# Graph attention over an edge list, one Trainium2 core: rows of one node and four edges, two to a partition, instead of rows of eight; the mixer's pair sums taken from K transposed times K

## The chip, the cores and the metric

The kernel runs on one core of one Trainium2 chip. The metric is the device time of one execution in microseconds (us).

## What is computed

A graph of N = 3125 nodes with F = 256 features has 50,000 pairs of nodes. Each pair is an edge in both directions, each node has an edge to itself, so there are E = 103,125 edges (`src`, `dst`), sorted by `dst`. The layer is a graph attention with a feed-forward net, a dense mixer over all nodes, and a mixture of experts:

```python
xn = layernorm(x)
q = xn @ Wq;  k = xn @ Wk;  v = xn @ Wv                  # 4 heads of 64
e = sum(k[src] * q[dst], per head) / sqrt(256)           # one number per edge and head
a = softmax of e over the edges that share a dst
ft = segment_sum(v[src] * a, dst)                        # then + xn, norm, ffn, norm
# mixer, 8 heads of 32: kn, qn normalised; vN = [1, v] / N
kv_mod[i, j, e] = sum_n kn[n, i] * kn[n, j] * vN[n, e]
y = 0.5 * sum_ij qn_i qn_j kv_mod[i, j] + scale^2 * qn @ kv + scale^4 * sum(vN)
y = y[..., 1:] / y[..., :1]
x = x + graph(xn) + mixer(xn)
x = x + experts(layernorm(x))                            # 8 experts, two per node
```

For the column e = 0 of `kv_mod`, where vN is 1/N, the sum over nodes of kn_i kn_j is an entry of K transposed times K.

## The kernel before

The work is in six stages, one after the other, each a block in which every engine has its own hand-written list of instructions, with semaphores between them. A stage begins when all engines have ended the one before.

**`stage_project`** (0 to about 100 us) normalises x, writes the table `kv_tab` (k and v of each node, 512 numbers, 2 KB a row) and `q_tab` to HBM, and works out on VectorE where each row of edges lies. The sorted edges are cut into blocks of L = 8. A *row* is a block of edges together with one node: where a block's eight edges reach into several nodes, it has a row for each, and the edges of other nodes are masked (`foreign`). This gives at most NB - 1 + N rows with NB = 12,891, in TILES = 126 tiles of 128 rows. The table `t3` in HBM says for each block which edges it holds.

**`stage_edges_and_mix`** (to 1443 us) goes over the tiles. For each tile n:

- SyncE loads 128 entries of `t3` (`load_blocks`, L2266 to L2270: one DMA of 127 rows and one of a single row) and 128 rows of q (`q_win`, L817).
- VectorE makes a comparison matrix (`compare`, L845), TensorE finds from it each row's block and node (`find`, L1219 to L1222), ScalarE turns these into the indices `idx`, the mask `foreign` and the spreading matrix (`settle`, L1110 to L1116). This runs AHEAD = 4 tiles ahead.
- GpSimd gathers k and v of the source nodes: 8 indirect DMAs per tile, one per edge slot of the 128 rows (L804, 256 KB each), into a ring of RING = 4 tiles. It waits for `idx` and, four tiles back, for the last reader of the ring's place.
- TensorE spreads q over the rows (`q_of_rows`, L1229). VectorE multiplies k by q in two halves of four slots (`times_q`, L855, into `prod`) and adds up per head (`add_up`, L862), masks (L869), takes the row's own maximum (L874) and subtracts it (L879). ScalarE takes exponentials (`exps`, L1121 to L1124).
- VectorE weighs v of four slots (`weigh`, L884), ScalarE v of the other four (`weigh_slot`, L1132, 16 instructions). VectorE adds its four by two folds (`fold` L892, `fold_on` L897), ScalarE's four by a reduction (`sum_act` L902), and the two sums (`fold_last` L910) into `part`, which goes to HBM (`parts`, 130 KB per tile).

Between these stand the mixer's instructions, cut into 477 micro-steps, four to a tile (`micro_steps`), so that they end seven tiles ahead of the last. Nine micro-steps are one window u of 125 nodes: first 26 rounds on K, V (`k_first`, `k_last`: for each head an outer product of pairs `kf_ps`, squared by ScalarE, L1164, and summed over the nodes by matmuls against v, L1269, and against a column of 1/N, L1270), then 13 steps of coefficients (`coef`), then 26 rounds on Q (L1324, L1344, L1346, squares at L1171). The order on each engine, the same for each tile, is written out at the end of its block: on VectorE

```python
for n in range(TILES + 1):
    # c = 0: times_q(n, 0)  times_q(n, 1)        c = 1: add_up(n, 0)  add_up(n, 1)
    # c = 2: keep_own(n)  weigh(n - 1)  top(n)  less_top(n)  fold(n - 1)
    # c = 3: compare(n + 5)  fold_on(n - 1)  sum_act(n - 1)  fold_last(n - 1)
```

(with three stretches of the micro-step `mix(n, c, ...)` around them).

**`stage_merge`** (to about 1587 us) first rescales rows of the same node to a common maximum, by scans along the rows (L1556 to L1575, one row of 128 numbers per tile and head), and then walks N_STEPS = TILES + NT - 1 = 150 steps, each a tile of rows added into a window of 125 nodes: SyncE loads the 130 KB of the tile (L1436), GpSimd scales them (L1528), ScalarE makes a selection matrix in two instructions (`mark`, L1512, L1515), TensorE multiplies (L1495, one fp32 product, two records), VectorE adds to `acc` (L1588). Every six steps VectorE loads six window numbers into registers.

`stage_graph_ffn`, the routing and `stage_experts` follow and are not touched, apart from the place of a buffer.

## Time and profile before

| | us |
|---|---|
| median of 3 executions | 2294.39 (2288.54 to 2297.39) |
| span of the profiled execution | 2291.0 |
| first gather of `stage_edges_and_mix` | 107.3 |
| last gather begins | 1423.8 |
| steps of `stage_merge`, first matmul to last add | 1467.3 to 1585.2 |

Of the profiled execution the page gives its span, 2291.0 us, and no separate time; what lies around the span is taken as the distance to the median of the executions, 3.4 us. The span is the time from its first instruction to its last. A busy share of an engine is its share of that span or of the window named; a DMA share is the mean over the core's 16 DMA engines.

### The profile page before, as it was taken

How to read it: one execution, taken by the hardware profiler on the slowest of the kernel's cores; microseconds unless marked ns; L12 is line 12 of the kernel's file. 1: busy time of each engine (PE TensorE's matmuls, PEld its weight loads, DVE VectorE, ACT ScalarE, POOL GpSimd, SP SyncE). 2: the span in 40 equal slices, each digit the busy share in tenths (PEclk: the TensorE clock that was granted, in tenths of full speed). 3: DMA queues.
4: the chain of work that ended last, by engine and by line, in shares of the span. 5: the costliest groups of instructions: out<-in, count | busy, mean ns of one | idle time of the engine just before them, and what ended most of it. 6: DMA issues, size and time to landing. Idle time of an engine off the chain costs nothing. (4 is left out here: it accounts for less than half of the span.)

```text
span 2291.0 us, 44322 instructions
## 1 busy us (share of the span) xinstructions
PE 1830.8 (80%) x12285; PEld 1291.9 (56%) x12285; DVE 1833.5 (80%) x3705; ACT 1525.4 (67%) x5228; POOL 1257.2 (55%) x1281
## 2 busy tenths in 40 slices
PE   7767788887786688787888771487999679999996
PEld 4433333333333566666666650244988579999995
DVE  7389999999999999999999999555899854444442
ACT  2267777778877587887888875687555255555553
POOL 0177777777777577777777776375000024444442
PEclk9879999889987688988989985698999789999998
DMA  8577777777777677777878787474001282222223
GB/s 229 182 230 232 231 230 235 233 224 228 228 226 228 182 230 239 235 234 237 237 232 242 226 243 211 138 206 119 15 29 32 89 280 38 35 35 36 37 37 77
DMA packets 213272, 394.34 MB, mean 172 GB/s; under 512 B 46354, under 2 KB 140637, under 8 KB 213005
## 3 DMA queue, kind: packets, MB, share of 16 engines
q0 software_dynamic: 91392, 278.99, 43.0%
q1 hardware_dynamic: 96848, 90.41, 13.3%
q10 hardware_dynamic: 24829, 22.64, 3.0%
q8 instruction: 78, 1.28, 0.2%
q14 instruction: 125, 1.02, 0.1%
HBM read 346.47 MB, written 48.65 MB: 172 GB/s over the span
## 5 line engine op out<-in xcount | busy, mean ns | idle before, releaser
L804 POOL DMA_INDIRECT ring<-kv_tab,idx x1008 | 981.0, 973 | 441.0 <-issue 297.6
L1132 ACT ACTIVATE act_val<-ring,act_val 128x64 f32<-128x64 f32 x2016 | 559.2, 398 | 51.0 <-DVE part L910 46.6
L855 DVE TENSOR_TENSOR prod<-ring,tile_bank 128x1024 f32<-128x1024 f32 x252 | 299.4, 1211 | 11.2 <-ACT tile_bank L1121 6.3
L862 DVE TENSOR_REDUCE score<-prod 128x16 f32<-128x1024 f32 x252 | 298.3, 1207 | 0.0
L2149 POOL DMA_INDIRECT x_sum<-e_yw,to_row x56 | 125.0, 2232 | 218.5 <-DVE e_yw L2175 197.2
L2134 POOL DMA_INDIRECT xr<-rows,from_row x56 | 57.6, 1029 | 291.2 <-issue 290.9
L2224 PE MATMUL e_h<-e_xT,e_now 128*128 128x128 f32 x1792 | 211.7, 277 | 0.8 <-DVE e_now L2165 0.8
L2224 PEld LDWEIGHTS e_h<-e_xT,e_now 128*128 128x128 f32 x1792 | 206.9, 194 | 1.3 <-DVE e_now L2165 1.2
L2239 PE MATMUL e_yps<-e_now,e_hT 128*128 128x256 f32 x896 | 202.5, 379 | 0.0
L2189 ACT ACTIVATE e_now<-e_w_all 128x2048 f32 x56 | 106.9, 1912 | 131.2 <-PE e_yps L2239 131.2
L2239 PEld LDWEIGHTS e_yps<-e_now,e_hT 128*128 128x128 f32 x896 | 166.2, 190 | 20.1
L2173 DVE TENSOR_TENSOR e_y<-e_yps,small 128x256 f32<-128x256 f32 x56 | 23.8, 425 | 189.2 <-PE e_yps L2239 182.0
L902 DVE TENSOR_REDUCE act_sum<-act_val 128x260 f32<-128x1040 f32 x126 | 154.5, 1226 | 14.2 <-ACT act_val L1132 14.1
L2197 ACT ACTIVATE e_hT<-e_h,small 128x128 f32<-128x128 f32 x448 | 127.6, 368 | 45.4 <-PE e_h L2224 45.4
L884 DVE TENSOR_TENSOR val<-ring,tile_bank 128x1024 f32<-128x1024 f32 x126 | 152.6, 1211 | 0.0
L1324 PE MATMUL bank_f<-u_T,pair 96*124 96x125 bf16 x800 | 90.1, 245 | 67.3 <-ACT xn_buf L1158 67.3
L1257 PE MATMUL bank_f<-pair,u_T 96*125 96x496 bf16 x200 | 89.6, 448 | 67.0 <-ACT u_T L681 34.3
L1257 PEld LDWEIGHTS bank_f<-pair,u_T 96*125 96x125 bf16 x200 | 28.4, 142 | 199.1 <-ACT phi L1164 77.1
L1229 PE MATMUL tile_bank<-q_win,spread 128*128 128x256 f32 x252 | 95.4, 466 | 38.2 <-DVE val L884 38.1
L1324 PEld LDWEIGHTS bank_f<-u_T,pair 96*124 96x124 bf16 x800 | 67.5, 149 | 102.9 <-ACT xn_buf L1158 74.6
L1270 PE MATMUL bank_f<-phi,one_col 125*32 125x496 f32 x200 | 118.1, 676 | 0.0
L1495 PE MATMUL step_ps<-scaled,hot 128*125 128x260 f32 x300 | 98.2, 436 | 20.7 <-DVE acc L1588 12.9
(425 smaller groups left out, 4794.0 us busy)
## 6 DMA issues: line engine op xcount, KB each, us to landing
loaded<-parts SPq DMA_DIRECT2D x150, 130.0 KB, 2.3
e_w_all<-L_ffn_W SPq DMA_DIRECT2D x16, 1024.0 KB, 12.2
parts<-part ACTq DMA_DIRECT2D x126, 130.0 KB
q_win<-q_tab SPq DMA_DIRECT2D x126, 128.0 KB
ring<-kv_tab,idx POOLq DMA_INDIRECT x1008
kv_tab<-kv_t SPq DMA_DIRECT2D x25, 224.0 KB
xn_buf<-x SPq DMA_DIRECT2D x25, 125.0 KB
x_sum<-x_buf SPq DMA_DIRECT2D x25, 125.0 KB
```

The costliest lines, as they stand in the source:

```text
L804: pool.indirect_dma_start(out=ring[:, n % RING, e, :], out_offset=None, in_=t.kv_tab, in_offset=bass.IndirectOffsetOnAxis(ap=idx[n % 6][:, ...
L855: dve.tensor_tensor(prod[half][:, :, :], ring[:, n % RING, at, 0:F], bcast(q_ps[n % 2].unsqueeze(1), 128, L // 2, F), ALU.mult).then_inc(q ...
L862: dve.tensor_reduce(score[:, at, :], prod[half][:, :, :].rearrange("p s (h d) -> p s h d", h=HG), AX.X, ALU.add).then_inc(reduced, 1)
L884: dve.tensor_tensor(val[n % 2][:, :, :, 0:DG], ring[:, n % RING, 0:L // 2, F:2 * F].rearrange("p s (h d) -> p s h d", h=HG), bcast(w_ps[n ...
L902: dve.tensor_reduce(act_sum[:, :], act_val[n % 2][:, :, :, :].rearrange("p h d s -> p (h d) s"), AX.X, ALU.add).then_inc(sum_ready, 1)
L1132: one = act.activation(act_val[n % 2][:, h, 0:DG, e - L // 2], ring[:, n % RING, e, F + h * DG:F + (h + 1) * DG], ACT.Copy, scale=act_val[ ...
L1270: pe.matmul(normT_ps[beyond, :], one_col[:, 1 - half:1 - half + DM], phi_k[h % 2], start=False, stop=last, skip_group_check=True).then_inc ...
L1324: mm = pe.matmul(qf_ps[k % 2][:, b, :], x.pair3[:, b * PB:(b + 1) * PB], q_.turned_parts[u % 2][:, k, 0:TP], start=True, stop=True)
L2149: pool.indirect_dma_start(out=t.x_sum, out_offset=bass.IndirectOffsetOnAxis(ap=to_row[:, n:n + 1], axis=0), in_=yw[n % 2][:, :], in_offset ...
L2197: gelu = act.activation(hT[j % 2][:, b, :], h_ps[j % 2][:, b, :], ACT.Gelu, bias=small[j][:, b:b + 1])
L2224: mm = pe.matmul(h_ps[j % 2][:, b, :], now1[j % 2][:, k, b * 128:(b + 1) * 128], xT[j % 2][:, k, :], start=(k == 0), stop=(k == FC - 1))
L2239: mm = pe.matmul(y_ps[j % 2][:, 0:F], hT[j % 2][:, b, :], now2[j % 2][:, b, :], start=(b == 0), stop=(b == HB - 1))
```

## The change

1. **Rows.** L is 4 and a new constant G is 2: a block has four edges, and a tile has 128 partitions with two rows each (G * L = 8 slots, as before). NB is 25,782, TILES = ceil((25,781 + 3,125) / 256) = 113, N_STEPS = 137. The gathers are 113 x 8 = 904 for 1008; their size is the same. The entries of `t3` are 40 bytes wide for 72, `load_blocks` issues four DMAs per tile for two, `q_win` is loaded twice per tile (two buffers for three), `parts` has 260 KB per tile.
2. **VectorE in a tile.** `times_q` writes its product over k in the ring. `compare` handles 256 rows in one instruction. `weigh` and `weigh_slot` now each weigh the four slots of one of the two rows, and all go to one buffer `val`, so that one fold over both rows (1040 numbers a partition) and a second (520) give `part`; `sum_act` and `fold_last` are gone. `fold` waits for ScalarE's four slots, and `weigh` waits for `where_read` and `q_ready[0]`, since the banks of PSUM are shared.
3. **Buffers in PSUM** for the q of the rows and for the weights `w_ps` are one per row and one, for two and two; `settle` is cut into `settle_rows` (c = 1) and `settle_nodes` (c = 2), `find` into `find_rows` and `find_nodes`.
4. **Mixer.** Every 16th slot takes two micro-steps (EXTRA = 16), so that 477 of them fit into 113 tiles. The matmuls against the column of 1/N (L1270) are gone; instead `gram_sums` adds K transposed times K of a window (two matmuls per window), and at the coefficients eight matmuls, two products and two reductions on VectorE make the pair sums of it.
5. **Merge.** The scans and their tables are 256 wide. Each step has two selections and two matmuls: the first row's by ScalarE (`mark`) and GpSimd as before, the second row's selection (`mark`) and scaling (`scale`) by VectorE.

```diff
@@ constants
-L = 8
+L = 4
+G = 2
-TILES = -(-(NB - 1 + N) // 128)
+TILES = -(-(NB - 1 + N) // (128 * G))
...
+def micros(n, c):
+    i = 4 * n + c
+    return range(i + i // EXTRA, i + 1 + (i + 1) // EXTRA)
@@ stage_project
+            def rows_of_edges():
+                for e in range(L):
+                    order(dve.tensor_tensor(split(edges[1])[:, :, e], split(edges[1])[:, :, e], blk_i[:, :], ALU.add))
@@ stage_edges_and_mix, gpsimd
-                for e in range(L):
-                    pool.indirect_dma_start(out=ring[:, n % RING, e, :], ...
-                                            ).then_inc(landed[n % RING * 2 + e // (L // 2)], 16)
+                for g in range(G):
+                    for e in range(L):
+                        pool.indirect_dma_start(out=ring[:, n % RING, g * L + e, :], ...
+                                                ).then_inc(landed[n % RING * 2 + g], 16)
@@ stage_edges_and_mix, vector
-                dve.tensor_tensor(prod[half][:, :, :], ring[:, n % RING, at, 0:F], bcast(q_ps[n % 2].unsqueeze(1), 128, L // 2, F),
-                                  ALU.mult).then_inc(q_read, 1)
+                k = ring[:, n % RING, g * L:(g + 1) * L, 0:F]
+                dve.tensor_tensor(k, k, bcast(q_ps[g].unsqueeze(1), 128, L, F), ALU.mult).then_inc(q_read[g], 1)
...
             def weigh(n):
                 dve.wait_ge(w_ready, n + 1)
+                dve.wait_ge(q_ready[0], min(n + 3, TILES))
+                dve.wait_ge(where_read, min(n + 2 + AHEAD, TILES))
...
             def fold(n):
-                dve.wait_ge(exp_ready, n + 1)
-                dve.tensor_tensor(v[:, 0:2, :], v[:, 0:2, :], v[:, 2:4, :], ALU.add).then_inc(folding, 1)
+                dve.wait_ge(act_val_ready, n + 1)
+                dve.tensor_tensor(v[:, :, 0:2 * FD], v[:, :, 0:2 * FD], v[:, :, 2 * FD:], ALU.add).then_inc(folding, 1)
...
-            def sum_act(n):
-                dve.tensor_reduce(act_sum[:, :], act_val[n % 2][:, :, :, :].rearrange("p h d s -> p (h d) s"), AX.X, ALU.add
-            def fold_last(n):
-                dve.tensor_tensor(part[n % 3][:, :], v[:, 0, :], act_sum[:, :], ALU.add).then_inc(folded, 1)
+                dve.tensor_tensor(part[n % 2][:, :, :], v[:, :, 0:FD], v[:, :, FD:2 * FD], ALU.add).then_inc(folded, 1)
@@ stage_edges_and_mix, tensor
+            def gram_sums(u, half):
+                at = slice(half * 128, (half + 1) * 128)
+                pe.matmul(gram_ps[:, half, :], k_.unit[u % 2][:, at], k_.unit[u % 2][:, at], start=False, stop=(u == NT - 1),
...
-                    pe.matmul(normT_ps[beyond, :], one_col[:, 1 - half:1 - half + DM], phi_k[h % 2], start=False, stop=last,
@@ stage_merge, tensor
-                pe.matmul(step_ps[n % 3][:, 0:FD], hot[n % 4][:, :], scaled[n % 3][:, :], start=True, stop=True
+                pe.matmul(step_ps[n % 3][:, 0:FD], hot0[n % 4][:, :], scaled0[n % 3][:, :], start=True, stop=False)
+                pe.wait_ge(hot1_ready, n + 1)
+                pe.wait_ge(scaled1_ready, n + 1)
+                pe.matmul(step_ps[n % 3][:, 0:FD], hot1[n % 4][:, :], scaled1[n % 3][:, :], start=False, stop=True
@@ stage_merge, vector
+            for n in range(N_STEPS):
+                if n % RUN == 0:
+                    window = numbers_of(t.step_w, n, mybir.EngineType.DVE, NT - 1)
+                if n + 1 < N_STEPS:
+                    mark(n + 1)
+                    scale(n + 1)
+                dve.wait_ge(step_ready, n + 1)
+                wait(dve, step_read, n)
+                at = t.acc[:, window[n % RUN], :]
+                dve.tensor_tensor(at, at, step_ps[n % 3][:, 0:FD], ALU.add).then_inc(step_read, 1)
```

How the order on VectorE moves, at two places. First a tile in the K rounds of `stage_edges_and_mix`. Before (`bank_l`, `slv_acc` and `u_` are the mixer's):

```order
L855 TENSOR_TENSOR prod1<-ring,tile_bank0 128x1024
L862 TENSOR_REDUCE score<-prod0 128x16
L862 TENSOR_REDUCE score<-prod1 128x16
L869 SCALAR_TENSOR_TENSOR own<-foreign4,score 128x32
L884 TENSOR_TENSOR val1<-ring,tile_bank0 128x16x64
L874 TENSOR_REDUCE m_all<-own 128x4
...
L879 TENSOR_TENSOR less0<-own,m_all 128x32
L892 TENSOR_TENSOR val1<-val1 128x520
L845 TENSOR_SCALAR later1<-iota,blocks3 128x128
L897 TENSOR_TENSOR val1<-val1 128x260
L902 TENSOR_REDUCE act_sum<-act_val1 128x260
L910 TENSOR_TENSOR part0<-val1,act_sum 128x260
```

and now:

```order
L883 TENSOR_TENSOR ring<-ring,tile_bank1 128x4x256
L888 TENSOR_REDUCE score<-ring 128x4x4
...
L897 SCALAR_TENSOR_TENSOR own<-marks,score 128x32
L914 TENSOR_TENSOR val0<-ring,tile_bank0 128x16x64
L902 TENSOR_REDUCE m_all<-own 128x8
L907 TENSOR_TENSOR less1<-own,m_all 128x32
L871 SCALAR_TENSOR_TENSOR later0<-place,blocks3 128x256
L922 TENSOR_TENSOR val0<-val0 128x2x520
L928 TENSOR_TENSOR part0<-val0 128x520
```

The six instructions from `less` on are four, and the first fold stands after `compare`. Second, the steps of `stage_merge`, before:

```order
L1588 TENSOR_TENSOR acc<-acc,step_ps2 125x260
L1431 TENSOR_LOAD step_w
L1588 ISA
L1588 TENSOR_TENSOR acc<-acc,step_ps0 125x260
L1588 ISA
L1588 TENSOR_TENSOR acc<-acc,step_ps1 125x260
```

and now (`hot` is the second row's selection, `scaled` its scaled parts, which lie in `g_ring`):

```order
L1497 TENSOR_LOAD step_w
L1667 TENSOR_SCALAR hot11<-iota,local 128x125
L1662 TENSOR_TENSOR scaled11<-g_ring,m_weights 128x260
L1683 ISA
L1683 TENSOR_TENSOR acc<-acc,step_ps0 125x260
L1667 TENSOR_SCALAR hot12<-iota,local 128x125
L1662 TENSOR_TENSOR scaled12<-g_ring,m_weights 128x260
```

VectorE has three instructions per step where it had one.

## Rows read from the trace of the kernel before

**Rows 1.** The page: busy time of each engine; the span in 40 slices of 57.3 us.

```profile
PE 1830.8 (80%) x12285; PEld 1291.9 (56%) x12285; DVE 1833.5 (80%) x3705; ACT 1525.4 (67%) x5228; POOL 1257.2 (55%) x1281
DVE  7389999999999999999999999555899854444442
POOL 0177777777777577777777776375000024444442
```

**Rows 2.** Windows of the edge stage: length, busy time and instructions per engine, PEclk, DMA share, GB/s.

```profile
200.00:466.00 266.00, 213.66 (x908) 83.84 (x909) 262.60 (x462) 205.92 (x770) 202.63 (x209) 0.91 0.79 232
486.00:700.00 214.00, 169.93 (x727) 67.69 (x727) 210.06 (x370) 165.36 (x615) 159.95 (x162) 0.90 0.77 224
730.00:794.00 64.00, 39.69 (x275) 33.56 (x275) 59.46 (x142) 32.28 (x133) 38.07 (x41) 0.55 0.66 194
794.00:1320.00 526.00, 428.75 (x4606) 338.04 (x4604) 509.03 (x882) 436.78 (x1628) 392.05 (x406) 0.88 0.79 234
1330.00:1380.00 50.00, 30.60 (x317) 23.46 (x313) 46.83 (x73) 38.10 (x148) 38.12 (x40) 0.82 0.81 244
```

**Rows 3.** One line of the source: the gathers, L804, and GpSimd's waits for the ring.

```profile
L804 POOL DMA_INDIRECT ring<-kv_tab,idx x1008: 940/946/1617, 107.3 to 1423.8; - x168
  issue: 297.6, 961
  ACT act_val L1132: 33.1, 27
```

**Rows 4.** Groups of VectorE: shapes, count, busy us, mean ns, idle before.

```profile
L855 DVE TENSOR_TENSOR prod<-ring,tile_bank 128x1024 f32<-128x1024 f32 x252 | 299.4, 1211 | 11.2 <-ACT tile_bank L1121 6.3 <-DMA ring<-kv_tab,idx 3.7 <-issue 0.6
L902 DVE TENSOR_REDUCE act_sum<-act_val 128x260 f32<-128x1040 f32 x126 | 154.5, 1226 | 14.2 <-ACT act_val L1132 14.1
L892 DVE TENSOR_TENSOR val<-val 128x520 f32<-128x520 f32 x126 | 87.2, 692 | 0.0
L910 DVE TENSOR_TENSOR part<-val,act_sum 128x260 f32<-128x260 f32 x126 | 53.4, 424 | 7.5 <-DVE act_sum L902 0.5 <-issue 0.4
L897 DVE TENSOR_TENSOR val<-val 128x260 f32<-128x260 f32 x126 | 52.9, 420 | 0.2
L845 DVE TENSOR_SCALAR later<-iota,blocks 128x128 bf16<-128x128 f32 x126 | 35.4, 281 | 3.0 <-PE tile_bank L1222 3.0
L1736 DVE SCALAR_TENSOR_TENSOR g_ring<-work,mv,gamma 125x256 f32<-125x256 f32 x25 | 11.6, 465 | 0.0
```

**Rows 5.** The stage before the first gather: a window of it.

```profile
20.00:60.00 40.00, 37.04 (x119) 19.81 (x118) 35.32 (x85) 9.03 (x25) 0.00 (x0) 0.96 0.75 227
```

**Rows 6.** The merge's steps: lines with min/median/max ns, first and last start; a window.

```profile
L1588 DVE TENSOR_TENSOR acc<-acc,step_ps x150: 424/425/427, 1468.7 to 1584.8; 125x260 f32 x150
L1528 POOL TENSOR_TENSOR scaled<-loaded,m_weights x150: 613/619/621, 1466.5 to 1582.0; 128x260 f32<-128x260 f32 x150
L1512 ACT ACTIVATE away<-iota,local x150: 365/385/401, 1466.2 to 1581.2; 128x125 f32<-128x125 f32 x150
...
1467.00:1585.20 118.20, 98.23 (x300) 48.60 (x300) 63.71 (x150) 102.92 (x299) 90.54 (x150) 0.95 0.68 190
```

**Rows 7.** Timeline of TensorE's weight loads in the merge: start, duration, instruction.

```profile
1522.20 0.29 PEld L1495 LDWEIGHTS step_ps<-scaled,hot 128*125 128x125 f32 x2 [0.28 <-issue]
1522.78 0.29 PEld L1495 LDWEIGHTS step_ps<-scaled,hot 128*125 128x125 f32 x2 [0.28 <-issue]
```

**Rows 8.** Groups of VectorE that price the second row's selection and the wider scans.

```profile
L394 DVE TENSOR_SCALAR entered<-thr,begin 128x126 f32<-128x126 f32 x1 | 0.3, 284 | 0.0
L1572 DVE TENSOR_TENSOR_SCAN run<-pen,start,m_rows 126x128 f32<-126x128 f32 x4 | 1.6, 467 | 0.0
```

**Rows 9.** Waits of ScalarE between 1000 and 1200 us: total, times, longest.

```profile
ACT phi L1171 <- PE bank_f L1324: 13.6, 7, 3.0
ACT tile_bank L1121 <- DVE less L879: 5.6, 6, 1.3
```

**Rows 10.** One line: SyncE's issue of the second DMA of `load_blocks`, ns.

```profile
L2270 SPq DMA_DIRECT2D blocks<-t x126: 346/1754/3867, 79.5 to 1354.3; - x126
```

More of the change, by code:

```diff
@@ L858, in add_up @@
-            def add_up(n, half):
-                at = slice(half * L // 2, (half + 1) * L // 2)
-                dve.wait_ge(q_read, 2 * n + half + 1)
+                dve.wait_ge(blocks_in[n % NBUF], G * 32 * (n // NBUF + 1))
+                wait(dve, local_found, n - 1)
+                dve.scalar_tensor_tensor(later[n % 2][:, :, :], place[:, :, :], float(128 * G * n),
+                                         bcast(blocks[n % NBUF][:, :, 2 * T3C:].bitcast(F32), 128, G, 128), ALU.add, ALU.is_ge
+                                         ).then_inc(compared, 1)
@@ L1038, in mix @@
                         onto_x(NT - 1)
+            def mix(n, c, stretch):
+                *whole, last = micros(n, c)
+                if stretch == 0:
+                    for i in whole:
+                        for part_of in range(3):
+                            mix_step(i, part_of)
+                mix_step(last, stretch)
             dve.memset(x.k_factor[:, :], SCALE)
@@ L1214, in _, with find_rows @@
+                    if c == 1 and n + AHEAD < TILES:
+                        settle_rows(n + AHEAD)
+            for j in range(2):
+                act.wait_ge(part_out[j], 16 * len(range(j, TILES, 2)))
         @block.tensor
         def _(pe):
[L1216 removed]
+            def find_rows(n):
                 pe.wait_ge(compared, n + 1)
[L1218 to L1222 removed]
```

598 lines of the change are left out of this document (324 added, 274 removed).

## The prediction

> **What bounds the kernel now.** I read the page first, to see which stages there are. VectorE is at nine tenths from the third slice to the 25th and GpSimd at seven tenths over the same slices, then both fall [rows 1]: the edge stage takes well over half of the span, and the other stages have other bounds. So the change is costed by stage.
>
> In the edge stage two engines are nearly equal, and the windows tell which one sets the pace. Between 200 and 466 us GpSimd does 209 gathers in 266 us, 1.273 us each, or 10.18 us for the 8 of a tile. This is almost its own pace: a gather has a median of 0.946 us, and 961 of 1008 have a gap of about 0.3 us before them which the profile puts down to nothing (297.6 us in all) [rows 3]. VectorE is busy in 98.7% of that window and falls behind a little with each tile, until the ring of four tiles is full. From then GpSimd is held back: 162 gathers in 214 us are 10.57 us a tile in the K rounds, 406 in 526 us are 10.36 us in the Q rounds, with VectorE at 98% and 97% [rows 2]. Between 730 and 794 us, the coefficients of the mixer, 41 gathers take 64 us, 11 us more than at 1.296 us. After the mixer's last step the tiles run at 10.0 us (40 gathers in 50 us), 1.25 us a gather, the gather's floor. So **VectorE bounds now by 2 to 4%, and GpSimd stands right behind it.** From 107.3 us, the first gather, to 1424.8 us, one gather after the last one's start [rows 3], it is 1317.5 us, 10.46 us a tile. TensorE (81%) and ScalarE (83%) have some air [rows 2].
>
> In the merge, 150 steps take 118.2 us, 0.79 us a step [rows 6]. ScalarE's two instructions per step (the first of them 0.385 us) leave it busy 103 of the 118 us; TensorE is busy 98, GpSimd 91, VectorE only 64. VectorE has 0.425 us of work per step.
>
> **The edge stage, GpSimd.** 104 gathers go. At 1.273 us they are worth 132 us; this is the floor of the gain if GpSimd keeps its pace and nothing else is slower. Since the tiles were at 10.46 us and not 10.18, more is to be had only as far as VectorE gets out of the way.
>
> **The edge stage, VectorE, per tile.** Gone: `sum_act` 1.226, `fold_last` 0.424, a fold of 520 numbers 0.692, one of 260 0.420, `compare` 0.281; together 3.043 us [rows 4]. Added: the fold of 1040 numbers, the fold of 520 (0.692) and `compare` on 256. From 260 to 520 numbers a fold grows by 0.272 us, so 1040 cost 0.692 + 0.544 = 1.236 us; `compare` is now a scalar-tensor-tensor on 256 numbers, which elsewhere takes 0.465 us. Together 2.393 us, **0.65 us less a tile**. The two products `times_q`, 1.211 us each [rows 4], keep their shape although they now write in place, and so do `add_up` and `weigh`. The mixer has 4.25 micro-steps per tile for 4. A quarter micro-step more is 0.1 us, an estimate: after the mixer's end the tiles run 0.4 to 0.6 us faster with VectorE less busy [rows 2], and a quarter of a fourth of VectorE's mixer work is of that order at most. The sum of durations also overstates what goes, since successive instructions overlap by some hundredths of a us and two of them go with their overlaps: I give 0.1 us back, a choice that no row here prices. That leaves 0.45 us: 10.57 becomes 10.1 in the K rounds, 10.36 becomes 9.9 in the Q rounds. Both are below GpSimd's 10.18, so **GpSimd becomes the bound**, by 1 to 3%.
>
> The value I take is 10.28 us a tile, 1% over GpSimd's pace, for a pair of engines that close will hold each other up at times: 113 x 10.28 = 1162 us. The bounds are 10.0 us (the tiles after the mixer) and 10.57 (the K rounds now). The jolt at the coefficients was 11 us; two products and two reductions of 512 numbers, 0.69 us each as the fold of 520 [rows 4], make it 3 us longer, but the ring is nearly empty behind a GpSimd that bounds, and three tiles of it take most: 5 us (0 to 14). Sum 1167 us for 1317.5: **150 us less**.
>
> Costed at nothing in this stage: the matmuls against the column of 1/N and the two per window that replace them (TensorE has idle time in the K rounds, busy 80% [rows 2]); the second `q_of_rows`, the two more matmuls of `find` (in the Q rounds TensorE goes from 81% to an estimated 92%; without that cover they would cost up to 1 us a tile); the second pair of loads of `t3`, whose second issue alone takes SyncE 1.75 us [rows 10], so some 4.5 us of 10.3 instead of 2.2; `q_win` and `parts`, some 0.26 MB more on 2.4 MB a tile, which takes the DMA share from 0.78 to about 0.87. The tail after the last gather, 18 us, stays.
>
> **The stage before.** `rows_of_edges` and wider tables add a few us to VectorE where it is 88% busy and TensorE 93% [rows 5]. Between 0 and 6 us, I take 3.
>
> **The merge.** Thirteen steps go. Each of the 137 has two products of TensorE. Weight loads of successive products come 0.58 us apart when nothing else holds them [rows 7], so TensorE needs 1.15 us a step: this is the lower bound, 158 us. VectorE gets a selection (0.284 us, a row of 126 numbers [rows 8]) and a scaling of 260 numbers (0.420 [rows 4]) ahead of its add (0.425 [rows 6]): 1.13 us a step, and every six steps the load of the window numbers, ahead of which nothing is prepared. Two engines at 1.15 and 1.13 us again. The upper bound is that GpSimd's scaling (0.619) stands in line with all three: 1.75 us. I take 1.30, near the lower end, since both rows there are of this same loop: 137 x 1.30 = 178 us for 118, **60 us more**. The 16 scans double their length, at 0.467 us now [rows 8] by at most 7.5 us, and three instructions on 512 numbers go to 1024: **8 us more** (5 to 10) before the first step.
>
> **Sum.** 2291.0 - 150 + 3 + 60 + 8 = 2212 us of span, and with the 3.4 us between span and median **2215 us**, 3.5% less.
>
> **A rule against the change.** GpSimd and VectorE each multiply two operands in SBUF in every merge step, where before VectorE's add had one of its two in PSUM. No row shows the two together: in the merge VectorE's add took 424 to 427 ns and GpSimd's scaling 613 to 621 ns, neither ever disturbed [rows 6]. The Trainium skill (SBUF — State Buffer, Who interferes with whom) says that a VectorE instruction with two SBUF inputs and a GpSimd instruction that reads SBUF share one port, and that the second waits for the whole of the first. By that rule alone the port would need 0.42 + 0.62 = 1.04 us a step and would hide under TensorE; it would cost where the waits line up, which is rival 2.
>
> **The rivals.**
>
> 1. *Lock step, slower than before.* `weigh(n - 1)` now waits for ScalarE's `settle_rows`, this for TensorE's `find_rows`, this stands behind `q_of_rows(n + 1, 0)`, which waits for VectorE's `times_q(n, 0)`; and `fold` waits for ScalarE's last slot. Behind a waiting `weigh` stand `top`, `less`, the exponentials and so ScalarE's next tile. ScalarE is busy 437 of 526 us in the Q rounds, 8.6 us a tile [rows 2], and waits another 0.7 us a tile for TensorE's outer products (13.6 us in 19 tiles [rows 9]); with a quarter micro-step and the wider `settle` that is about 9.9. For it: all three engines are above 90% then. Against it: the waits fall in another third of the tile than the work they wait for, and now ScalarE waits only 5.6 us in 200 for `less`. It decides from (1317.5 - 71 - 5) / 113 = 10.98 us a tile; at 11.6, two hand-offs of some 0.6 us on top of 10.3, the stage takes 1316 us and the whole 2291 - 2 + 71 + 3 = **2363 us**. Chance 0.09.
> 2. *The merge in line.* VectorE and GpSimd take turns, 1.75 us a step: 240 us, 62 more than forecast: **2277 us**. Durations of the two scalings well above 0.42 and 0.62 us would show it. Chance 0.10.
> 3. *Transfers hold the gathers.* In the windows the gathers' own time is 0.97 us on average where the median is 0.946, and some reach 1.617 [rows 3], at a DMA share of 0.78. With 0.87 more of them may. 10.8 us a tile is 1220 us, 58 more: **2273 us**. Against it: at 0.81 the share was highest when the gathers were fastest, 1.25 us each [rows 2]. Chance 0.10.
> 4. *Clean.* Tiles at GpSimd's 10.18 us, 1150 us, no jolt, and TensorE alone in the merge, 158 us: 37 us better, **2178 us**. Chance 0.13.
>
> That the change doesn't do what it says can be left out: the counts of tiles and steps are constants in the program.
>
> **The numbers.** The forecast has the remaining 0.58. The range 2165 to 2295 holds cases 2, 3 and 4 with some room, and leaves out rival 1 and the ends of the unknowns. A measurement of this kernel tells 0.5%, 11 us, from no change. Faster by more than that (below 2283): the forecast, rival 4 and about three fifths of rivals 2 and 3, 0.84. Within it: the rest of these, 0.07. Slower: 0.09.
>
> **What would show each step.** Edge stage: 904 gathers, 8 of them in about 10.2 to 10.3 us, with GpSimd seldom waiting for anything but the 0.3 us, VectorE now waiting for gathers (products idle before on ring landings), folds of 1.24 and 0.69 us, the stage shorter by some 150 us. Merge: TensorE or VectorE above 85% over 137 steps of 1.3 us, VectorE's scaling at 0.42 us. The forecast is wrong if VectorE waits for ScalarE at `weigh` or `fold` by more than half a us a tile, if the gathers' mean rises above 1.05 us, or if the merge's step is above 1.6 us.

## The result, and the profile after

The changed kernel takes **2466.35 us** (median, 2463.6 to 2469.2) against 2295.89 us before: a ratio of **1.0755, 95% interval 1.0738 to 1.0771**. It is 7.6% slower, where 3.5% faster was forecast. The profiled execution has a span of 2464.2 us, 173.2 us more than before. By stage, with the forecast beside it:

| Stage | before | after | change | forecast |
|---|---|---|---|---|
| start to first gather | 107.3 | 120.2 | +12.9 | +3 |
| first gather to last | 1317.5 | 1426.4 | +108.9 | -150 |
| to the merge's first product | 42.2 | 53.4 | +11.2 | +8 |
| steps of the merge | 118.2 | 161.0 | +42.8 | +60 |
| after it | 705.8 | 703.2 | -2.6 | 0 |

So the merge is better than forecast, and the edge stage misses by 259 us. The whole misses the 2215 us of the forecast by 251 us. The page shows where: busy time by engine, then the span in 40 slices of 61.6 us (rows of before: [rows 1]).

```profile
PE 1951.8 (79%) x12642; PEld 1393.1 (57%) x12642; DVE 1757.3 (71%) x3576; ACT 1475.4 (60%) x4781; POOL 1187.8 (48%) x1164
DVE  7378899999998667765666677788799974444442
POOL 0077777777775646544555556155200003444442
```

Up to the 12th slice VectorE is at eight or nine tenths and GpSimd at seven, nearly as before. From the 14th on, where the mixer turns to the queries, VectorE is at five to seven tenths and GpSimd at four to six for ten slices: neither is the bound there. The same windows as in [rows 2] give the sizes:

```profile
200.00:466.00 266.00, 232.04 (x865) 99.44 (x865) 244.01 (x403) 205.10 (x721) 200.68 (x201) 0.91 0.82 247
486.00:700.00 214.00, 186.41 (x735) 80.91 (x736) 202.74 (x336) 173.02 (x608) 163.55 (x162) 0.96 0.82 248
730.00:794.00 64.00, 41.83 (x269) 33.88 (x269) 53.24 (x124) 27.29 (x106) 37.81 (x38) 0.57 0.65 194
794.00:1320.00 526.00, 353.55 (x3523) 270.39 (x3518) 341.54 (x551) 320.45 (x1108) 283.84 (x283) 0.79 0.61 182
```

In the K rounds 201 gathers in 266 us are 10.59 us a tile and 162 in 214 are 10.57: GpSimd sets the pace there (in the first of these windows it waits 4.8 us in all for the ring), but at 10.6 and not at its 10.18 of before. In the Q rounds 283 gathers in 526 us are **14.87 us a tile**, with VectorE busy 65% (before: 10.36 us and 97%) and the clock granted to TensorE at 0.79 for 0.88. That is the loss. One line of the source, the gathers and what GpSimd waited for ([rows 3] before):

```profile
L827 POOL DMA_INDIRECT ring<-kv_tab,idx x904: 940/946/3992, 120.2 to 1545.6; - x181
  issue: 392.1, 850
  ACT val L1160: 232.3, 51
```

Waits for a free place in the ring are 232.3 us for 33.1. The waits of the other engines, each with total, times and longest (TensorE, VectorE twice, SyncE), lead back to the cause:

```profile
PE tile_bank L1273 <- DMA q_win<-q_tab: 193.9, 22, 13.4
...
DVE val L914 <- ACT marks L1137: 134.4, 28, 9.5
DVE val L922 <- ACT val L1160: 91.0, 49, 6.4
...
SPq L846 <- DVE x_buf L1029: 327.0, 23, 19.7
```

VectorE waits for ScalarE at `weigh` and at `fold`, the very chain that rival 1 named; but the chain's head is TensorE, waiting 22 times for a **q window that has not been loaded**, once in most of the 26 rounds on Q. SyncE issues that load, and SyncE waits 23 times for `onto_x` before it may load the next tile of x. SyncE's timeline in one Q round (start, duration, line), and TensorE's row beside it:

```profile
1009.41 0.32 SPq L846 DMA_DIRECT2D xn_buf<-x  x1
1010.70 0.29 SPq L2365 DMA_DIRECT2D blocks<-t  x1
1011.19 2.15 SPq L2366 DMA_DIRECT2D blocks<-t  x1
1014.35 0.27 SPq L2365 DMA_DIRECT2D blocks<-t  x1
1014.81 0.80 SPq L2366 DMA_DIRECT2D blocks<-t  x1
1016.63 1.49 SPq L842 DMA_DIRECT2D q_win<-q_tab  x2
1018.91 0.29 SPq L2365 DMA_DIRECT2D blocks<-t  x1
```

```profile
1022.03 1.22 PE L1273 MATMUL tile_bank<-q_win,spread 128*128 128x256 f32 x2 [8.03 <-DMA q_win<-q_tab]
```

`load_x` stands in SyncE's program ahead of the next tile's `load_q`. It got free at 1009.4, the two pairs of `blocks` took it to 1015.6, the q windows were issued from 1016.6 on, and TensorE's product began at 1022.03, after 8.03 us in which it stood still. A tile's own loads take SyncE 8.2 us (1010.70 to 1018.91) in which it waits for nobody. Before, the same wait was there and cost TensorE 0.2 us in all: q windows were loaded three tiles ahead. Its row in the trace of before:

```profile
SPq L821 <- DVE x_buf L1012: 301.2, 23, 24.1
```

The merge, a window and its VectorE lines ([rows 6] before), and the two folds:

```profile
1600.00:1761.00 161.00, 138.83 (x548) 92.97 (x548) 137.06 (x410) 93.73 (x272) 85.19 (x136) 0.99 0.80 235
```

```profile
L1662 DVE TENSOR_TENSOR scaled<-g_ring,m_weights 128x260 f32<-128x260 f32 x137 | 57.5, 420 | 0.0
L1605 POOL TENSOR_TENSOR scaled<-g_ring,m_weights 128x260 f32<-128x260 f32 x136 | 85.3, 628 | 73.2 <-PE step_ps L1571 72.7 <-DMA g_ring<-parts 0.5
```

```profile
L922 DVE TENSOR_TENSOR val<-val x113: 1221/1241/1276, 149.2 to 1566.0; 128x1040 f32<-128x1040 f32 x113
L928 DVE TENSOR_TENSOR part<-val x113: 677/699/702, 150.5 to 1567.3; 128x520 f32<-128x520 f32 x113
```

A step is 161.0 / 137 = 1.175 us, shorter than the 1.30 of the forecast. The folds cost 1.24 and 0.70 us, as estimated from [rows 4].

### The profile page after: what moved, and what is told of

The parts are those of the page before. It is cut to its first block and busy times, and to the rows that moved or that the text cites. A ratio compares the mean times of both kernels' runs of the same rounds, so it can differ in the third digit from the quotient of the medians.

```text
span 2464.2 us, 45710 instructions
## 1 busy us (share of the span) xinstructions
PE 1951.8 (79%) x12642; PEld 1393.1 (57%) x12642; DVE 1757.3 (71%) x3576; ACT 1475.4 (60%) x4781; POOL 1187.8 (48%) x1164
## 3 DMA queue, kind: packets, MB, share of 16 engines
q14 instruction: 130, 1.06, 0.1%
## 5 line engine op out<-in xcount | busy, mean ns | idle before, releaser
L827 POOL DMA_INDIRECT ring<-kv_tab,idx x904 | 918.5, 1016 | 625.3 <-issue 392.1
L1160 ACT ACTIVATE val<-ring,val 128x64 f32<-128x64 f32 x1808 | 475.7, 336 | 25.7 <-DVE part L928 22.3
L1273 PE MATMUL tile_bank<-q_win,spread 128*128 128x256 f32 x452 | 175.0, 475 | 224.6 <-DMA q_win<-q_tab 193.9
L883 DVE TENSOR_TENSOR ring<-ring,tile_bank 128x1024 f32<-128x1024 f32 x226 | 269.1, 1212 | 15.2 <-DMA ring<-kv_tab,idx 7.8
L888 DVE TENSOR_REDUCE score<-ring 128x16 f32<-128x1024 f32 x226 | 267.8, 1208 | 0.0
L914 DVE TENSOR_TENSOR val<-ring,tile_bank 128x1024 f32<-128x1024 f32 x113 | 137.7, 1218 | 134.7 <-ACT marks L1137 134.4
L1273 PEld LDWEIGHTS tile_bank<-q_win,spread 128*128 128x128 f32 x452 | 87.7, 224 | 246.4 <-DMA q_win<-q_tab 198.5
L922 DVE TENSOR_TENSOR val<-val 128x1040 f32<-128x1040 f32 x113 | 139.9, 1238 | 91.5 <-ACT val L1160 91.0
L1605 POOL TENSOR_TENSOR scaled<-g_ring,m_weights 128x260 f32<-128x260 f32 x137 | 85.9, 628 | 95.0 <-PE step_ps L1571 72.7
L1135 ACT ACTIVATE idx<-tile_bank 128x8 int32<-128x8 f32 x113 | 18.3, 162 | 154.1 <-PE tile_bank L1260 154.1
```

The costliest lines, as they stand in the source:

```text
L827: pool.indirect_dma_start(out=ring[:, n % RING, g * L + e, :], out_offset=None, in_=t.kv_tab, in_offset=bass.IndirectOffsetOnAxis(ap=idx[n ...
L883: dve.tensor_tensor(k, k, bcast(q_ps[g].unsqueeze(1), 128, L, F), ALU.mult).then_inc(q_read[g], 1)
L888: dve.tensor_reduce(score[:, :, g, :], ring[:, n % RING, g * L:(g + 1) * L, 0:F].rearrange("p s (h d) -> p s h d", h=HG), AX.X, ALU.add).t ...
L914: dve.tensor_tensor(val[n % 2][:, 0, :, :, 0:DG], ring[:, n % RING, 0:L, F:2 * F].rearrange("p s (h d) -> p s h d", h=HG), bcast(w_ps.unsq ...
L922: dve.tensor_tensor(v[:, :, 0:2 * FD], v[:, :, 0:2 * FD], v[:, :, 2 * FD:], ALU.add).then_inc(folding, 1)
L1160: one = act.activation(val[n % 2][:, 1, e, h, 0:DG], ring[:, n % RING, L + e, F + h * DG:F + (h + 1) * DG], ACT.Copy, scale=val[n % 2][:, ...
```

## The experiments

Ratios are those on record, each to the kernel before in runs beside it (medians of 2290.8 to 2293.9 us, 2295.9 beside the changed kernel); they are not exactly the quotients of the medians. Where kernels of different batches differ by a few us, the ratios compare them better than the times. "Late x" is the changed kernel with the first edit below; "three repairs" is late x with the first blocks loaded by GpSimd and the merge reading 12 numbers at a time.

| Kernel | us | ratio, 95% interval |
|---|---|---|
| changed | 2466.35 | 1.0755 (1.0738 to 1.0771) |
| late x | 2269.94 | 0.9893 (0.9869 to 0.9918) |
| third q window, x load left | 2286.2 | 0.9953 (0.9929 to 0.9978) |
| before, two q windows | 2390.64 | 1.0419 (1.0396 to 1.0443) |
| late x, rows in 112 + 15 | 2267.65 | 0.9880 (0.9857 to 0.9903) |
| late x, 32 rows of q | 2264.94 | 0.9892 (0.9859 to 0.9925) |
| late x, first blocks by GpSimd | 2248.27 | 0.9830 (0.9804 to 0.9855) |
| late x, merge reads 12 | 2251.78 | 0.9849 (0.9825 to 0.9874) |
| before, mixer part alone | 2291.24 | 1.0002 (0.9992 to 1.0012) |
| **three repairs** | **2237.75** | **0.9758 (0.9739 to 0.9776)** |
| + third q window | 2238.05 | 0.9758 (0.9739 to 0.9777) |
| + one more addition | 2311.64 | 1.0084 (1.0058 to 1.0109) |
| + reductions, slots innermost | 2327.81 | 1.0164 (1.0145 to 1.0183) |
| + second fold moved | 2245.16 | 0.9793 (0.9774 to 0.9813) |
| before, its two repairs | 2292.62 | 1.0000 (0.9989 to 1.0012) |

### SyncE's line: the x load, the third buffer, and the kernel before with two

```diff
@@ sync
-                            if kind == "q" and k == 0 and u + 1 < NT:
+                            if kind == "q" and k == 7 and u + 1 < NT:
                                 load_x(u + 1)
```

> The changed kernel with one edit: SyncE issues the load of the x tile of mixer round u+1 at step 7 of query round u instead of step 0, so its wait on VectorE's addition (step 4) is over when SyncE gets there. Theory A (SyncE's line: the x load waits 327 us in all, 23 times, with the next tile's two q window loads queued behind it, and two q buffers leave no slack): the wait of TensorE for q_win, 193.9 us in the changed kernel, falls under 30 us, the query rounds go from 14.9 us per tile to 11 to 12, and the time from 2466 us to about 2280 (2250 to 2330). Theory B (the two sub-tiles now go through TensorE, ScalarE and VectorE in lock step, and the late window is only where that shows): the query rounds stay above 14 us per tile and the time stays within 30 us of 2466.

It took 2269.94 us, 196 us less. The Q rounds and the gathers of this run (windows, then the group of the gathers: busy us, mean ns, idle before):

```profile
800.00:1280.00 480.00, 415.88 (x4513) 321.71 (x4511) 433.62 (x703) 404.85 (x1415) 366.03 (x355) 0.93 0.83 251
```

```profile
L827 POOL DMA_INDIRECT ring<-kv_tab,idx x904 | 922.4, 1020 | 424.5 <-issue 383.7
```

Now 355 gathers in 480 us are 10.82 us a tile, the ring's wait is 39.6 us, and no wait for `q_win` is left among TensorE's longest. Theory A holds; lock step alone (rival 1) does not, with the same instructions in the same order on TensorE, ScalarE and VectorE.

```diff
@@ x load left where it was
-        q_win = [s.sb(f"q_win{i}", [128, G, F]) for i in range(2)]
+        q_win = [s.sb(f"q_win{i}", [128, G, F]) for i in range(3)]
@@ sync
-                if n + 2 < TILES:
-                    load_q(n + 2)
+                if n + 3 < TILES:
+                    load_q(n + 3)
...
```

The lines left out are the indices and waits of the third buffer, and two small buffers (`own`, `y_inv`) that move to make room.

> The changed kernel with three q window buffers in place of two (loads three tiles ahead), the x load left where it was; y_inv and own move to free columns to make room. Theory A (a late load is what holds the query rounds): the third buffer gives each load one tile more, some 10 us, about the length of the waits (13.4 us the longest for q_win), so most of them go and the time comes near that of the run with the x load moved, 2270 to 2340 us. Theory B (lock step): no change, within 30 us of 2466.

2286.2 us (2268 to 2293 in nine runs): the same loss goes by the other way, most of it.

```diff
@@ kernel before
-        q_win = [s.sb(f"q_win{i}", [128, F]) for i in range(3)]
+        q_win = [s.sb(f"q_win{i}", [128, F]) for i in range(2)]
...
-                    load_q(n + 3)
+                    load_q(n + 2)
...
```

> The kernel before with two q window buffers in place of three and loads two tiles ahead. Theory A: its SyncE waits 301 us for the same x addition, 23 times, so the depth alone brings the waits for q_win there too: the query rounds lengthen and the time goes from 2295 to 2350 to 2450 us. If the doubled loads of the change are needed besides, the time stays within 20 us of 2295.

2390.64 us, 97 us more, and its trace has the changed kernel's wait:

```profile
PE tile_bank L1229 <- DMA q_win<-q_tab: 133.2, 20, 10.8
```

So the depth alone brings the wait. The changed kernel, with its longer line of loads, has more of it (193.9 us for 133.2); how much of that is due to the doubled loads, no run separates.

### Transfers and the long gathers

With the x load moved, a tile is 1228.8 / 113 = 10.87 us: 8.16 of gathers (mean 1.020), 2.35 of gaps of 0.3 us (383.7 us less the 118 ahead of the first gather), 0.35 of waits for the ring. Before it was 7.79 (mean 0.973), 2.36 and 0.26. The gathers themselves are longer, as rival 3 had it. Two runs ask for its cause, the transfers.

```diff
@@ load_blocks, on late x
-        sp.dma_start(to[1:128, g, :], t.t3[ds(first, 127), :])...
+        sp.dma_start(to[16:128, g, :], t.t3[ds(first + 15, 112), :])...
+        sp.dma_start(to[1:16, g, :], t.t3[ds(first, 15), :])...
```

> The run with the x load moved, and the 127 rows of blocks loaded as 112 rows and 15 rows, so that SyncE issues three DMAs for a sub-tile where it issued two. If the 127-row loads crowd few DMA engines and so stretch the gathers (mean 1.011 us in the pair rounds, 0.946 median), GpSimd's 10.6 us per tile there fall by 0.1 to 0.5 us, and the time by 5 to 40 us against that run. If it is only one more DMA on a full SyncE queue, the time is the same or up to 20 us more.

2267.65 us, no difference: the windows of the K rounds are alike (201 gathers in 266 us), and two more issues a tile on SyncE show no cost once its wait is out of the way.

```diff
@@ load_q, on late x; q rows 32 to 127 of a window are left out from the third tile on
-                    sp.dma_start(q_win[n % 2][:, g, :], t.q_tab[ds(first, 128), :])...
+                    rows = 128 if n < 2 else 32
+                    sp.dma_start(q_win[n % 2][0:rows, g, :], t.q_tab[ds(first, rows), :])...
```

> The run with the x load moved, but from the third tile on each q window load brings 32 rows instead of 128 (the other 96 rows of the buffers keep what the first loads left; what is left out is the load of q rows 32 to 127 of a window). It takes 192 KB of some 2.6 MB a tile off the DMA engines. Theory (rival 3 of the prediction: transfers stretch the gathers, mean 1.020 us each where the median is 0.946): the mean falls to 0.96 to 0.99 us, the tile by 0.2 to 0.5 us, the time by 20 to 50 us. Rival (the gathers are long by themselves, by what they move): mean 1.01 or more, time within 8 us of 2270.

The DMA share between 200 and 466 us fell from 0.82 to 0.77 and the gathers did not notice:

```profile
200.00:466.00 266.00, 231.22 (x864) 99.03 (x862) 242.72 (x402) 204.61 (x721) 199.69 (x201) 0.91 0.77 228
```

```profile
L827 POOL DMA_INDIRECT ring<-kv_tab,idx x904 | 924.4, 1023 | 423.6 <-issue 382.6
```

Mean 1.023, time the same (2264.94 us, ratio 0.9892 for 0.9893). Fewer transfers do not shorten the gathers: the cause that rival 3 gave is wrong. What does is in the timeline of late x, GpSimd first and VectorE below:

```profile
869.75 0.95 POOL L827 DMA_INDIRECT ring<-kv_tab,idx  x1 [0.30 <-issue]
871.01 1.57 POOL L827 DMA_INDIRECT ring<-kv_tab,idx  x1 [0.30 <-issue]
872.89 0.95 POOL L827 DMA_INDIRECT ring<-kv_tab,idx  x1 [0.30 <-issue]
```

```profile
870.53 1.23 DVE L922 TENSOR_TENSOR val<-val 128x1040 f32<-128x1040 f32 x1
871.80 0.70 DVE L928 TENSOR_TENSOR part<-val 128x520 f32<-128x520 f32 x1
```

The gather that starts during the fold ends at 872.58, 0.08 us after the second fold. Between 800 and 1000 us, 24 of 147 gathers take over 1.05 us, and 16 of these lie beside both folds. The folds are VectorE's longest instructions of this stage with both operands in SBUF (the next take 0.42 us).

### The folds and the gathers

```diff
@@ on late x: fold (g = 0) and fold_on (g = 1) become
+                dve.tensor_reduce(part[n % 2][:, g, :], v[:, g, :].rearrange("p (s x) -> p x s", s=L), AX.X, ALU.add)
```

> The run with the x load moved, and the two folds of a tile (additions of two operands in SBUF, 1.24 and 0.70 us) replaced by two reductions over the four slots, one for each sub-tile (one operand in SBUF, 1040 numbers each, some 1.2 us each as the products of as many numbers). Theory (shared port): in the trace of the run with the x load moved, the long gathers end 0.05 to 0.1 us after a fold or the fold behind it has ended (gather 871.01 to 872.58, folds 870.53 to 871.76 and 871.80 to 872.50); GpSimd waits for VectorE's additions with two SBUF operands. Without them the gathers' mean falls from 1.020 to 0.96 or 0.97 us, the tile by 0.3 to 0.5 us, the time by 15 to 50 us against 2270, although VectorE works 0.4 us more a tile. Rival: the coincidence means nothing (both wait for the same tile's data); then the gathers keep their 1.02 us and the time stays or rises by up to 15 us.

This run (2791.5 us) and the next three were taken together, beside a kernel before of 2854 us where all other batches have 2291 to 2296, and in their traces TensorE, VectorE and ScalarE stood still together for up to 9.3 us at a time; so their times answer nothing here, and durations are compared within the group alone. The gathers' mean was 1.001 us with the folds (the first of the next three) and **0.951 us** with the reductions. But a reduction over slots 1040 bytes apart took 1.93 us, not 1.2, and VectorE had 1.9 us more a tile.

> The changed kernel with three edits that each were run with the x load moved: x load later, first five blocks loaded by GpSimd, step numbers of the merge read 12 at a time. If their gains add up (22 and 18 us against 2270), 2225 to 2238 us; if they overlap, 2240 to 2250.

> The same three edits, and the reductions in place of the folds, the first of them no longer waiting for ScalarE's slots. Shared port theory: 15 to 50 us under the run with the three edits alone, 2180 to 2215 us. Rival: the same as that run, or up to 15 us more.

> All of these and the third q window buffer. With the x load moved a late q window held TensorE for no more than a few us, so the third buffer is worth nothing: within 6 us of the run without it. If the shorter tiles bring SyncE's line back to the critical path, 10 to 30 us less.

They took 2727.8, 2798.4 and 2791.5 us: in this group the kernel with the reductions is slower than the one with the folds, and the third window changes 7 us, less than the runs scatter. The first was repeated in a later batch, in which the kernel before took 2290.8 us. It has the late x load and two repairs whose own runs stand further down; the kernels after it have all three and one edit more.

> The kernel of best_a again (x load later, first five blocks by GpSimd, step numbers 12 at a time), beside a kernel before of the usual time. If the three gains add up, 2225 to 2238 us; if they overlap, 2240 to 2250.

2237.75 us, within the 2225 to 2238 expected: the three gains add up to within 8 us (2269.94 - 21.7 - 18.2 = 2230). Its gathers have a mean of 1.027 us.

```diff
@@ fold_on: one more addition ahead of the second fold
+                dve.tensor_tensor(v[:, :, 2 * FD:3 * FD], v[:, :, 2 * FD:3 * FD], v[:, :, 3 * FD:], ALU.add)
```

> The kernel of best_a2 with one more addition of 520 numbers, two operands in SBUF, ahead of the second fold of each tile (its result is not used; some 0.70 us). VectorE is busy 243 of 266 us in the pair rounds, so it has 0.9 us a tile to spare. Shared port theory: GpSimd's gathers wait for this addition too, their mean rises from 1.02 to 1.06 to 1.10 us, and the time by 0.3 to 0.7 us a tile, 35 to 80 us. Rival (the gathers are long by themselves, and VectorE hides the addition): mean within 0.01 us, time up to 15 us more.

74 us more, 0.65 us a tile for an addition of 0.70 us: next to nothing of it is hidden. The gathers' mean over the kernel rose from 1.027 to 1.049 us, less than the 1.06 to 1.10 expected. In the K rounds (three repairs, then this kernel):

```profile
200.00:466.00 266.00, 232.44 (x872) 100.09 (x873) 242.91 (x402) 205.63 (x722) 202.15 (x200) 0.91 0.82 246
```

```profile
200.00:466.00 266.00, 224.37 (x831) 95.37 (x830) 248.30 (x411) 197.77 (x693) 202.61 (x192) 0.91 0.78 237
```

A gather there takes 202.61 / 192 = 1.055 us for 1.011, which is 0.35 us of the tile's 0.44. In the Q rounds (800 to 1260 us) the tile grows by 0.75 us and the gathers by only 0.09 of it; there VectorE's lateness holds the ring (GpSimd's waits for a place in it go from 11.0 to 35.0 us in this window). So the lock is only a part of the 74 us. VectorE's busy time, 243 of 266 us, looked like 0.9 us a tile to spare, and it was not.

```diff
@@ slots innermost
-        val = [s.sb(f"val{i}", [128, G, L, HG, DG + 1]) for i in range(2)]
+        val = [s.sb(f"val{i}", [128, G, HG, DG + 1, L]) for i in range(2)]
@@ fold (g = 0), fold_on (g = 1)
...
+                dve.tensor_reduce(part[n % 2][:, g, :], val[n % 2][:, g, :, :, :].rearrange("p h d s -> p (h d) s"), AX.X, ALU.add)
```

> The kernel of best_a2 with the slots innermost in val and a reduction over them for each sub-tile in place of the folds, as the kernel before did for ScalarE's half at 1.226 us (slots 1040 bytes apart cost 1.93 us). VectorE: 2.45 us a tile for 1.94, so some 10.2 us of work in a tile of 10.6, if the weighing keeps its 1.21 us with slots as the inner step; ScalarE 16 times 0.06 us more. Shared port theory: gathers' mean 0.95 to 0.97 us, the tile between 10.2 and 10.5 us, the time 10 to 40 us less. Rival: the gathers keep 1.02 us and the time stays or rises by up to 20 us. If the weighing gets slower with its strided output, the time rises although the gathers get shorter.

```profile
L826 POOL DMA_INDIRECT ring<-kv_tab,idx x904 | 865.4, 957 | 449.9 <-issue 260.7
...
L916 DVE TENSOR_TENSOR val<-ring,tile_bank 128x1024 f32<-128x1024 f32 x113 | 227.1, 2010 | 6.3 <-ACT marks L1140 5.8
...
L924 DVE TENSOR_REDUCE part<-val 128x260 f32<-128x1040 f32 x113 | 138.7, 1227 | 0.0
```

The gathers are short again, 0.957 us, 63 us less of GpSimd's time in all; and the weighing, which now writes every fourth number, takes 2.01 us for 1.22. VectorE, busy 96% between 200 and 466 us, becomes the bound at over 11 us a tile, and the whole is 90 us slower. The last case of the expectation came in.

```diff
@@ no instruction more: the second fold between the next tile's products
                 mix(n, 0, 1)
+                if n > 1:
+                    fold_on(n - 2)
...
-                if old:
-                    fold_on(n - 1)
...
```

> The kernel of best_a2 with one move: the second fold of a tile stands between the two products times_q of the tile after the next instead of right behind the first fold (and ScalarE stores the part two steps later). No instruction is added. Shared port theory: a gather that was held by both folds, 1.24 and 0.70 us back to back, is now held by one at a time; the gathers' mean falls from 1.027 to 0.98 to 1.01 us and the time by 10 to 30 us against 2238. Rival (the total of the additions counts, not that they are adjacent): mean and time the same within 0.01 and 8 us.

A miss for both cases of the expectation: mean 1.058 us, 31 ns more, and 7 us more time. Between 300 and 500 us 36 of 147 gathers are long, where it was 23 of 149 with the folds side by side. Apart, each fold catches a gather of its own; together they catch one. The ends tell the same. With the folds apart, 141 of the kernel's 192 long gathers end 0.8 us after a fold has ended: a gather that starts during a fold gets on when the fold is over. With the folds side by side, 54 of 146 end 0.1 us after the second. So the lock is shown (gathers 0.957 without the folds and 1.02 to 1.06 with them, in the slow group 0.951 and 1.001), and what it costs the whole kernel is shown from above only, by the added addition: no version without folds kept VectorE's work the same.

> The kernel of best_a2 and three q window buffers. With the x load moved, late windows hold TensorE for a few us at most: within 6 us of best_a2.

2238.05 us, as expected.

### The start, the merge, the mixer

```diff
@@ stage_project: SyncE's load_blocks go to GpSimd, with semaphores of their own
+            pool.wait_ge(fixed_out, 4 * 16)
+            pool.wait_ge(first_known, 1)
+            for n in range(AHEAD + 1):
+                load_blocks(pool, t, n)
```

> The run with the x load moved, and the first five tiles' blocks loaded by GpSimd, which is idle in the projection stage, instead of by SyncE between its stores of kv_tab and q_tab. Theory: the first gather came 13 us later in the changed kernel than before because SyncE spends about 6 us a projection tile there (two loads of a first block, each some 2 us with its register load, and the stores behind them; VectorE waits 14.3 us for stores of kv_t), so the first gather comes at 108 to 112 us instead of 120.9 and the time falls by 8 to 13 us against that run (2270). Rival: the 13 us come from the wider tables on VectorE; then the first gather stays at 118 us or later and the time within 4 us.

22 us less. The first gather comes at 106.0 us, before even that of the kernel before; VectorE's wait for the stores of `kv_t`, 14.1 us in the changed kernel, is gone:

```profile
L826 POOL DMA_INDIRECT ring<-kv_tab,idx x904: 941/947/3062, 106.0 to 1328.3; - x181
```

14.9 us are at the start. Much of the rest is the batch: in the one of this run, the kernel with 32 rows of q, whose gathers are as long as those of late x, took 2264.94 us, 5 us less than late x in its own. Against that it is 17 us.

```diff
@@ stage_merge
-    RUN = 6
+    RUN = 12
```

> The run with the x load moved, and the merge reads its step numbers 12 at a time instead of 6. Theory: the merge is bound by VectorE, not by TensorE; between two reads a step takes some 0.9 us, and each read (1.09 us median, 23 of them) stands in VectorE's line with nothing prepared behind it. Twelve fewer reads take 12 to 18 us off the merge (161 us) and off the time. Rival: TensorE's two products set 1.15 us a step, as the prediction had it; then the time stays within 4 us of 2270.

18 us less (13 against the kernel with 32 rows of q in the same batch), 10.7 of them in the merge's steps, a little under the 12 expected (late x, then this kernel; TensorE's products from first to last):

```profile
1404.20:1563.90 159.70, 137.61 (x547) 92.20 (x546) 136.09 (x408) 92.79 (x269) 84.15 (x135) 0.99 0.81 237
```

```profile
1396.20:1545.20 149.00, 138.38 (x547) 92.32 (x546) 136.74 (x409) 92.71 (x269) 84.30 (x135) 0.99 0.85 254
```

The same work in less time, at 1.09 us a step for 1.17: the reads stand in VectorE's line and TensorE waits for them. TensorE's 1.15 us a step is no floor.

> The kernel before with the mixer half of the change alone: K transposed times K on TensorE, two matmuls a window, in place of eight matmuls a window against the column of 1/N, and the pair sums worked out from it once. The prediction costed it at nothing: VectorE bounds the pair rounds, TensorE is 80% busy there, so within 8 us of 2294. If TensorE held VectorE back after all (it waits 50.6 us for slv_acc at the outer products, and VectorE works for it), up to 25 us less; if the longer step at the coefficients shows, up to 5 us more.

No change (1.0002). The mixer half of the change, costed at nothing, costs nothing on the kernel before.

> The kernel before with the two repairs that it has a place for: the x load at step 7, the merge's step numbers read 10 at a time instead of 6. With three q window buffers its late x load costs nothing, and its merge is bound by ScalarE (103 of 118 us) in its 0.79 us a step: within 8 us of 2291. If the reads hold its merge too, 10 us less.

No change either (1.0000). What these two repairs win, they win from the change. The third, first blocks by GpSimd, was not tried on the kernel before, whose first gather comes at 107.3 us for 106.0; with that said, **the repaired change is 53 us, 2.4%, faster than the kernel before**.

## Why the prediction was wrong

- **The step that failed** is in the list of what was costed at nothing: "the second pair of loads of `t3` ... so some 4.5 us of 10.3 instead of 2.2; `q_win` and `parts`", of which only the megabytes were counted. SyncE was treated as busy time and not as a line. Its own issues take 8.2 us a tile; ahead of them, once a round, stands a wait of up to 19.7 us; and the change took one of three buffers from the load behind it. The 4.5 us for the loads of `t3` was near (4.9 us in the timeline); what hangs on their place was not asked. All three facts, two buffers for three, two pairs of loads for one, and a SyncE that waits 301 us for `onto_x`, stood in the diff and the trace of before, and no term put them together. With the wait moved out of the way the kernel is 196 us faster.
- **Rival 1** had the direction, and at 2363 us 148 of the 251 us that the forecast missed, by accident. Its chain (weigh, settle_rows, find_rows, q_of_rows) is what the waits show, with other numbers: 12.6 us a tile over the stage, for its 11.6, and 14.87 in the Q rounds. But it had `q_of_rows` wait for `times_q`; it waits for a DMA. With the DMA on time, GpSimd waits 0.35 us a tile for the ring, for 0.26 before the change: the longer chain by itself shows there as a tenth of a us.
- **The edge stage at 10.28 us a tile.** With the x load moved it is 10.87, 1229 us for 1167. GpSimd did become the bound, as said, but "its own pace" of 10.18 was read beside additions of 0.69, 0.42 and 0.42 us; beside folds of 1.24 and 0.70 us a gather takes 1.02 us and not 0.97. That is 0.4 us of the 0.69 over 10.18; the waits for the ring, which 10.18 has hardly any of, are the 0.35, and the gaps are a little shorter. VectorE's own terms were right to 0.05 us (folds 1.238 and 0.696 for 1.236 and 0.692, `compare` 0.418 for 0.465). The sum counted each engine's instructions and left out that they lengthen each other's. **Rival 3** had the sign and the size (10.8 us a tile) and the wrong cause: the DMA share came to 0.82 and not to 0.87, and 0.77 in its place changed nothing.
- **The rule against the change** was weighed for the merge, where it cost little: the scaling took GpSimd 0.628 us for 0.619. It was not asked about the edge stage, where it holds: the gathers take their indices from SBUF (`idx`). The rule (the Trainium skill, SBUF — State Buffer, Who interferes with whom) names exactly this pair, a VectorE instruction with two SBUF inputs and a GpSimd instruction that reads SBUF, and the runs agree with it: 1.027 us with such folds, 0.957 without. Of the making of DMA descriptors, the section infers that such an addition leaves it alone. Here the gather as a whole is not left alone; which part of it waits, reading the indices or writing descriptors, no run tells.
- **The stage before**, +3 (0 to 6), measured +12.9: the wider tables were counted, and SyncE's five double loads between the stores, near 6 us a projection tile, were not. The same omission as above. With these loads on GpSimd the first gather comes at 106.0 us, so the wider tables show no cost there.
- **The merge**, 1.30 us a step, bounds 1.15 and 1.75: 1.175, 43 us more instead of 60. The choice near the lower end was right, its reason only partly: VectorE's reads of the window numbers held it, which the prediction named and did not price, and with half of the reads a step takes 1.09, under the lower bound. Ahead of the first step it was 11 us more for 8 (5 to 10).
- **The mixer** at nothing: right, by a run of its own.

## What to carry to other kernels

An engine that only issues DMAs is a line like any other: write down, in microseconds, the wait and what stands behind it up to the load that somebody needs, and compare the sum with the time that the buffers give, which is their depth in tiles times the time of a tile; a change that thins the buffers and lengthens the line at once must be summed as one. When instructions of one engine grow, look at what the neighbour's instructions cost while they run, not only at their own length. And when a rule is found that speaks against a change, ask it of every stage, not of the one that brought it to mind.

## What the runs showed of the hardware

- A gather of 0.946 us grew to up to 4.0 us beside VectorE's additions of two SBUF operands. Held by one addition it ended 0.8 us after the addition's end (141 of 192 long gathers with the folds apart); held by two back to back, 0.1 us after the end of the second. Two such additions back to back held one gather; apart they held two (mean 1.027 and 1.058 us).
- VectorE's cost depends on where the numbers lie: a reduction of 1040 numbers over four neighbours took 1.23 us, over four numbers 1040 bytes apart 1.93; the weighing of 1024 numbers took 1.22 us written in a row and 2.01 us at steps of 16 bytes. The Trainium skill (SBUF — State Buffer, Door 1: The DMA port swizzle) has lines of 16 bytes in SBUF, with a penalty for each access that crosses to a new one; the two prices fit it, and no run here tried a step under 16 bytes against it.
- SyncE's issue of a single row of 40 bytes right behind the 127 rows took 1.5 us in the median (225 to 3264 ns), five times the issue of the 127 rows ahead of it (0.29).
